# Two attention layers over adjacency graphs: q, k and v products cut into pieces of five and four matmuls, and TensorE's items dealt anew over the steps

## What is computed

```python
h = relu(layernorm(x))                         # before each layer
# layer 0
q, k, v = heads(h @ Wq + bq), heads(h @ Wk + bk), heads(h @ Wv + bv)
s = q @ k.T / sqrt(32) + beta * adj
p = softmax(where(adj > 0, s, -9e15))
x = x + p @ v
# layer 1
q, k, v = heads(h @ Wq.T), heads(h @ Wk.T), heads(h @ Wv.T + bv)
s = q @ k.T * 384 ** -0.5 + (adj + adj)
p = nan_to_num(softmax(where(any(s != 0), s, -inf)))
x = x + (p @ v) @ Wo.T + bo
```

## Time and profile before

| | us |
|---|---|
| profiled execution, as run | 1990.03 |
| its span in the profile | 1988.3 |
| median of three runs | 1988.66 |
| PE, busy | 1900.5 |
| DVE, busy | 1828.6 |
| ACT, busy | 1676.5 |
| POOL, busy | 913.0 |

### The profile page before, as it was taken

How to read it: one execution, slowest core, us unless ns; L and a number is a source line. 1 busy time by engine, 2 the same in 40 slices (tenths; PEclk the granted TensorE clock), 3 DMA queues, 4 the chain that set the end, 5 groups by cost and what they waited for, 6 DMA issues and landing times.

```text
span 1988.3 us, 50014 instructions
## 1 busy us (share of the span) xinstructions
PE 1900.5 (96%) x18336; PEld 1229.1 (62%) x18336; DVE 1828.6 (92%) x3989; ACT 1676.5 (84%) x4275; POOL 913.0 (46%) x1114
## 2 busy tenths in 40 slices
PE   5999999999999999997999999999999999999998
PEld 3566666666666666664666666666666666666665
DVE  5999999999999999997989999999999999999984
ACT  4999999999999999997977887887887888887885
POOL 5465556556655455561353334343343334343331
PEclk9999999999999999998999999999999999999999
DMA  3888999988899898889787788778787788777884
GB/s 134 197 215 220 228 225 234 229 228 223 230 226 230 231 233 226 226 224 225 201 218 198 187 215 222 189 202 210 193 216 194 189 221 211 199 200 202 203 200 113
DMA packets 104723, 415.92 MB, mean 209 GB/s; under 512 B 27008, under 2 KB 31104, under 8 KB 104480
## 3 DMA queue, kind: packets, MB, share of 16 engines
q1 hardware_dynamic: 77728, 305.24, 63.3%
q0 software_dynamic: 26752, 107.49, 18.4%
HBM read 88.61 MB, written 25.17 MB: 57 GB/s over the span
## 4 chain that ended last, share of the span: by engine, by line
PE 49%; DVE 25%; ACT 11%; DMA 6%; SPq 5%; issue 3%; POOL 1%; DVEq 0%; POOLq 0%
DVE s L393 13%; PE sc L248 11%; PE ring L281 11%; DVE pt L406 10%; PE out L340 9%; PE ring L309 6%; ACT s L516 6%; SPq L204 5%; PE ring L265 5%; PE ring L288 4%; DMA pk<-pt 4%; ACT xin L523 2%; PE ring L274 2%; ACT pl L548 1%; PE ring L300 1%
## 5 line engine op out<-in xcount | busy, mean ns | idle before, releaser
L516 ACT ACTIVATE s<-s,nmax 128x512 f32<-128x512 f32 x1536 | 1094.9, 726 | 157.6 <-DVE nmax L393 157.5
L393 DVE CUSTOM_DVE_ANT_0 s<-sc,bias 128x512 f32<-128x512 f32 x1536 | 968.0, 686 | 53.0 <-PE sc L248 25.2
L406 DVE STREAM_TRANSPOSE pt<-s 128x2048 f32<-128x2048 f32 x285 | 656.8, 2304 | 0.0
L248 PE MATMUL sc<-k,q 32*128 32x512 f32 x3072 | 439.9, 642 | 51.0 <-DVE nmax L393 36.2
L516 ACT ACTIVATION_READ_ACCUMULATOR s<-s,nmax 128x1 f32 x1536 | 311.0, 202 | 0.0
L340 PE MATMUL out<-pk,v 128*32 128x192 f32 x6080 | 287.2, 330 | 6.0 <-DMA pk<-pt 6.0
L340 PEld LDWEIGHTS out<-pk,v 128*32 128x32 f32 x6080 | 178.8, 110 | 140.4 <-issue 87.4
L288 PE MATMUL ring<-wv,hT 128*128 128x384 f32 x1152 | 236.3, 349 | 0.0
L281 PE MATMUL ring<-hT,wq 128*128 128x512 f32 x864 | 228.1, 409 | 1.5 <-DVE hT L421 1.5
L281 PE MATMUL ring<-hT,wk 128*128 128x512 f32 x864 | 228.0, 408 | 0.0
L248 PEld LDWEIGHTS sc<-k,q 32*128 32x128 f32 x3072 | 121.5, 184 | 164.0 <-DVE nmax L393 82.8
(11 more groups left out here) (93 smaller groups left out, 1891.4 us busy)
## 6 DMA issues: line engine op xcount, KB each, us to landing
pk<-pt SPq DMA_DIRECT2D x1520, 192.0 KB, 4.9
bias<-in_adj POOLq DMA_DIRECT2D x32, 1024.0 KB, 10.3
res<-in_x POOLq DMA_DIRECT2D x16, 768.0 KB, 7.4
x_between<-res POOLq DMA_DIRECT2D x16, 768.0 KB, 4.5
xin<-x_between POOLq DMA_DIRECT2D x16, 768.0 KB, 10.1
res<-x_between POOLq DMA_DIRECT2D x16, 768.0 KB, 10.6
xin<-in_x POOLq DMA_DIRECT2D x15, 768.0 KB, 9.8
out_x<-res POOLq DMA_DIRECT2D x15, 768.0 KB, 7.0
```

The costliest lines, as they stand in the source:

```text
L248: mm = nc.tensor.matmul(m.sc[:, j, :], m.q[rows, s % 2, P * t:P * (t + 1)], m.k[rows, s % 2, :], start=True, stop=True)
L393: nc.vector.tensor_tensor_reduce(out=m.s[:, t % 2, j, :], in0=m.sc[:, j, :], in1=m.bias[g % 2][:, t, :], scale=s_scale[layer], scalar=3.0e ...
L406: nc.vector.transpose(out=to, in_=m.s[:, t % 2].rearrange("p j (i a e) -> p (j i) a e", a=QUADS, e=HD)).then_inc(turned, 1)
L516: nc.scalar.activation(tile, tile, ACT.Exp, bias=m.nmax[s % 2][:, t, j:j + 1], scale=-1.0, accum_out=m.sums[s % 2][:, t, j:j + 1]).then_in ...
```

## The change

`qk` and `v` get a first piece each, `qk_first` and `v_first`, with places of their own: five of the nine matmuls (`PIECE` = 5). The second piece does the other four into the same bank and then signals. `ring_places` gives the bank to the first piece; it waits for the bank's last reader and the inputs, the second piece waits for nothing. ACT, DVE and POOL skip first pieces. All places of PE's items are new, in both layers, and so are the load steps. The whole of it, with the table of places cut to some rows (layer 0, then layer 1):

```diff
 PLACES = ({
-    "qk": (-2.90, -1.90, 1.10, 2.10, 4.27, 6.10),
-    "v": (-3.50, -0.50, 0.50, 3.50),
+    "qk_first": (-2.93, -1.89, 1.20, 2.11, 5.20, 6.24),
+    "qk": (-2.41, -1.82, 1.38, 2.11, 5.98, 6.33),
+    "v_first": (-3.53, -0.56, 0.80, 3.51),
+    "v": (-3.13, -0.20, 1.71, 3.75),
...
-    "post": (17.50, 17.60, 18.50, 20.60),
+    "post": (17.77, 18.36, 20.07, 20.27),
...
-    "pv": (5.20, 6.70, 8.32, 9.20, 10.70, 12.32, 13.20, 14.70, 16.32),
-    "spread": (7.30, 12.30, 16.61),
+    "pv": (6.31, 7.28, 8.12, 9.31, 10.69, 12.12, 13.86, 14.69, 16.12),
+    "spread": (7.30, 11.62, 14.21),
...
+FIRST = {"qk_first": "qk", "v_first": "v"}
+PIECE = 5
...
-X_STEP, ADJ_STEP, RES_STEP, BIAS_STEPS = 8, (3, 6), (6, 2), (5, 7, 8, 10)
+X_STEP, ADJ_STEP, RES_STEP, BIAS_STEPS = 9, (1, 5), (6, 3), (3, 5, 6, 8)
...
-    ringed = [x for x in OPENING + steps + CLOSING if x[0] != "pv" and x[:2] != ("post", GRAPHS - 1)]
+    ringed = [x for x in OPENING + steps + CLOSING if x[0] not in ("pv", *FIRST.values()) and x[:2] != ("post", GRAPHS - 1)]
     for n, x in enumerate(ringed):
+        result = (FIRST.get(x[0], x[0]), *x[1:])
         slot[x], replaces[x] = n % RING, held[n % RING]
-        held[n % RING] = x
+        slot[result], held[n % RING] = n % RING, result
...
+            def piece(kind):
+                return range(PIECE) if kind in FIRST else range(PIECE, 3 * DT)
...
-                if replaces[kind, g, i]:
+                if replaces.get((kind, g, i)):
...
-                if kind == "qk":
-                    pe.wait_ge(done["hT"], nth("hT", g, DT - 1))
-                    if i < 2 and g % B == 0:
-                        pe.wait_ge(weights_split[i], layer_of(g) + 1)
+                if kind in ("qk_first", "qk"):
+                    if kind == "qk_first":
+                        pe.wait_ge(done["hT"], nth("hT", g, DT - 1))
+                        if i < 2 and g % B == 0:
+                            pe.wait_ge(weights_split[i], layer_of(g) + 1)
                     w, a = (m.wq, m.wk)[i % 2], i // 2
-                    for n, (t, x, y) in enumerate(halves):
+                    for n in piece(kind):
+                        t, x, y = halves[n]
...
-                mm.then_inc(ready[kind], 1)
+                if kind not in FIRST:
+                    mm.then_inc(ready[kind], 1)
```

More of the change, by code:

```diff
@@ L49 @@
 PLACES = ({
-    "hT": (-4.50, -4.40, -4.30),
-    "qk": (-2.90, -1.90, 1.10, 2.10, 4.27, 6.10),
-    "v": (-3.50, -0.50, 0.50, 3.50),
-    "tp": (3.31, 3.32, 3.33, 3.34, 7.31, 7.32, 7.33, 7.34, 11.31, 11.32, 11.33, 11.34),
-    "pv": (5.20, 6.20, 8.20, 9.20, 10.20, 12.20, 13.20, 14.20, 16.20),
-    "post": (17.50, 17.60, 18.50, 20.60),
[L56 to L62, removed]
-    "pv": (5.20, 6.70, 8.32, 9.20, 10.70, 12.32, 13.20, 14.70, 16.32),
-    "spread": (7.30, 12.30, 16.61),
-    "post": (17.50, 17.60, 18.50, 20.50),
-})
+    "hT": (-4.46, -4.36, -4.26),
+    "qk_first": (-2.93, -1.89, 1.20, 2.11, 5.20, 6.24),
+    "qk": (-2.41, -1.82, 1.38, 2.11, 5.98, 6.33),
+    "v_first": (-3.53, -0.56, 0.80, 3.51),
+    "v": (-3.13, -0.20, 1.71, 3.75),
+    "tp": (3.41, 3.48, 3.49, 3.50, 7.33, 7.39, 7.48, 7.48, 11.08, 11.18, 11.26, 11.27),
+    "pv": (5.26, 6.96, 8.47, 9.36, 10.96, 12.28, 13.12, 14.95, 16.20),
+    "post": (17.77, 18.36, 20.07, 20.27),
+}, {
+    "hT": (-4.50, -4.41, -4.30),
+    "qk_first": (-2.92, -1.93, 1.05, 2.07, 4.69, 6.07),
+    "qk": (-2.75, -1.82, 1.25, 2.42, 5.12, 6.10),
+    "v_first": (-3.45, -0.53, 0.74, 3.46),
+    "v": (-3.40, -0.07, 1.20, 3.82),
+    "sums": (0.30, 4.30, 9.76),
+    "zero": (2.09, 5.92, 10.64),
+    "tp": (3.31, 3.32, 3.33, 3.34, 7.31, 7.32, 7.33, 7.34, 11.31, 11.32, 11.33, 11.34),
+    "pv": (6.31, 7.28, 8.12, 9.31, 10.69, 12.12, 13.86, 14.69, 16.12),
+    "spread": (7.30, 11.62, 14.21),
+    "post": (17.30, 17.58, 18.08, 20.41),
+})
+FIRST = {"qk_first": "qk", "v_first": "v"}
+PIECE = 5
 OUT_STEP = ((9, 9, 9), (9, 9, 9))
 STATS_STEP, RELU_STEP = (-12, -8), (-7, -6)
-X_STEP, ADJ_STEP, RES_STEP, BIAS_STEPS = 8, (3, 6), (6, 2), (5, 7, 8, 10)
+X_STEP, ADJ_STEP, RES_STEP, BIAS_STEPS = 9, (1, 5), (6, 3), (3, 5, 6, 8)
 def place(kind, g, i):
@@ L90 @@
     IN_STEP.setdefault(math.floor(at), []).append(x)
-OPENING = [x for kind in ("hT", "qk", "v") for at, x in ITEMS if at < 0 and x[0] == kind]
+OPENING = [x for kinds in (("hT",), ("qk_first", "qk"), ("v_first", "v")) for at, x in ITEMS if at < 0 and x[0] in kinds]
 PER_CHUNK = {"tp": HC, "pv": PARTS, "spread": 1}
@@ L274, in item @@
                         mm = nc.tensor.transpose(to[:, P * t:P * (t + 1)], m.xin[:, t, P * i:P * (i + 1)], m.ident[:])
-                if kind == "qk":
-                    pe.wait_ge(done["hT"], nth("hT", g, DT - 1))
-                    if i < 2 and g % B == 0:
-                        pe.wait_ge(weights_split[i], layer_of(g) + 1)
+                if kind in ("qk_first", "qk"):
[3 more added lines that the diff above has]
+                            pe.wait_ge(weights_split[i], layer_of(g) + 1)
                     w, a = (m.wq, m.wk)[i % 2], i // 2
-                    for n, (t, x, y) in enumerate(halves):
+                    for n in piece(kind):
+                        t, x, y = halves[n]
                         mm = nc.tensor.matmul(to, w[y][:, t, P * a:P * (a + 1)], m.hT[x][:, t, :], start=n == 0, stop=n == 3 * DT - 1)
-                if kind == "v":
-                    if i == 0:
+                if kind in ("v_first", "v"):
+                    if kind == "v_first" and i == 0:
                         pe.wait_ge(done["hT"], nth("hT", g, DT - 1))
@@ L358, in _ @@
                 item(*x)
-                if x == ("v", 0, 0):
+                if x == ("v_first", 0, 0):
                     scores(0, 0, 0)
@@ L415, in item @@
             def item(kind, g, i):
-                if kind == "pv":
+                if kind == "pv" or kind in FIRST:
                     return
@@ L531, in item @@
             def item(kind, g, i):
-                if kind == "pv" or (kind, layer_of(g)) == ("post", 1):
+                if kind == "pv" or kind in FIRST or (kind, layer_of(g)) == ("post", 1):
                     return
```

## The result

| | before | after |
|---|---|---|
| median of the runs, us | 1989.87 (4 runs) | 1974.49 (4 runs, 1972.13 to 1975.07) |
| profiled execution, us | 1990.03 | 1972.13 |

The ratio is 0.9922, its 95% interval 0.9906 to 0.9937. A second set of five runs gave 1974.1 and the same ratio. The forecast of 1989 us and no change was wrong: the kernel is faster by far more than the interval. 1974.49 does lie inside the stated range, 1973 to 2004, but near its lower edge. In a later set one execution of the kernel before took 7751 us, for a reason that nothing here shows; it is left out of every comparison.

What follows compares the result with a forecast made beforehand. It took PE to bound layer 1's steps 4 to 11, and chains over PE, ACT and DVE layer 0. 1990.03 + 5.4 - 5.5 = 1989.9; with the median 1.4 below the profiled run, 1989 us, range 1973 to 2004.

Steps and rivals of the forecast that it cites:

- Sum +0.35 us per graph: Layer 1, steps 4 to 11, PE the bound: cuts and block ends add 0.35 us per graph, +5.4 us (0 to +16).
- the mark that the text set for its refutation: Layer 1: a graph period under 63.3 us would refute the predicted price of the cuts.
- Cuts, +0.1, +0.2 and +0.1: Layer 1: cutting q at the scores +0.1 us, k around a post-product +0.2, v around the spread +0.1.
- zero, +0.1: Layer 1: the small "zero" transpose moves from between full-array blocks to ahead of the scores, +0.1 us per graph.
- post, -0.15: Layer 1: the post-product no longer ends ahead of P-times-v, -0.15 us per graph.
- A spread that leaves step 4 and one that comes into step 11: Layer 1: two spread blocks on PE, 0.41 us each, one leaving and one entering, claimed to change nothing.
- rival 2: Only changes between kinds of block count: 33 stretches for 35 in layer 1, -10.6 us, about 1979; chance 0.12.
- rival 1: Layer 0 gives all: free cuts, waits for h and DMA gone, -0.9 us in 15 graphs, 1976; chance 0.21.
- Rivals 3: Layer 1: each cut and new end costs 0.33, +16 us, with -3 from layer 0: 2002; chance 0.21.
- Rival 4: Layer 1: the residual load comes late, some 1.2 us per graph, +19 us, 2008; chance 0.08.
- Layer 0: Moving q from step 4 to 5 ends ACT's and DVE's waits: -0.35 us per graph, -5.5 us (0 to -14).
- Load steps: Adjacency, bias, x and residual loads at new steps: claimed to cost nothing, covered by about 1 us of slack.

## Why the prediction was wrong

**The step that failed: "Sum +0.35 us per graph", the price of cuts and ends in layer 1, +5.4 us.** Measured: -0.17 to -0.18 a graph; the period of 63.31 is 0.01 above the mark that the text set for its refutation, and far from the 63.6 to 64.1 that it expected. By its terms:

- *Cuts, +0.1, +0.2 and +0.1; zero, +0.1; post, -0.15.* The chains give them all as 0. What costs is the first full-array block behind another kind: q 2.28 there and 2.10 behind a spread, Wo 4.07 and 3.87, Wo with six 2.13 and 1.94, v 1.77 to 1.79 and 1.58 (the first two behind sums or P times v, the last behind Wo). That is 0.18 to 0.21 each time, and scores and P times v take 1.07, 1.44 and 1.01 wherever they stand. Pieces on both sides of the scores pay it once more in q and save it in Wo. I read the prices from starts in the timeline of overlapping blocks, and put them at ends: 0.33 for one ahead of another kind, which is too much, and up to 0.24 where the kind does not change, which is nothing. Whether the 0.19 belongs to the way into full-array work or out of it the sums can't tell, since there are as many ways out as in; the chain, with its modelled ends, puts it at the entry. From the chain through graph 27 before:

```profile
1675.90 0.59 PE ring L300 x4
1676.49 2.10 PE ring L281 x9
...
1705.78 1.77 PE ring L288 x9
```

- *A spread that leaves step 4 and one that comes into step 11, taken as nothing.* The one that leaves gives 0.41 (0.59 less the 0.18 that q then pays itself), and by that steps 5 to 8 became shorter. The one that comes stands inside v's product, ahead of the scores that DVE takes in step 1, and costs 0.44 there. The cut itself costs nothing: v's pieces take 0.97 and 0.71, the whole v 1.67 before. The chain after, and then the row of before:

```profile
1635.34 0.97 PE ring L302 x5
1636.31 0.44 PE ring L314 x4
1636.74 0.71 PE ring L302 x4
```

```profile
1651.97 1.67 PE ring L288 x9
```

So the two spreads did cancel, nearly. The 0.44 less the 0.19 of the next term is the 0.24 by which step 0 grew, and 0.41 less 0.24 is the 0.17 of the period.

- *v from step 9 to step 8* was in no term at all. Its entry, 0.19, is what is left as layer 1's gain, and put back to step 9 it cost 0.34 of 0.36 us a graph (0.21 for its entry, 0.13 for the sums behind it). Moved alone in the kernel before it brought nothing (63.49), though PE held the chain there too: DVE was just behind, and in that run took the chain over from step 9 on.

```profile
1693.12 2.15 PE ring L309 x6
...
1696.44 2.23 DVE pt L406
```

So the Trainium skill, page TensorEngine Tiling (Array Packing), section Key Properties, was the better guide: a change of tiling mode drains the engine. These rows agree for the way into full-array work, by 0.18 to 0.21, and show no price for the other changes of kind but 0.13 at the sums. Over a graph the entries into full-array work fell from 14 to 12, on the chain of steps 4 to 11 from 9 to 8. So of the two changes fewer that **rival 2** counted, one entry counts, 0.19 instead of 0.66; the sign was right, the price a third. That its 1979, and the 1976 of **rival 1**, come near the measured time is luck: layer 0 gave 0.48 a graph and not the 0.9 of rival 1, and graph 17 and the load steps stood in neither. Rivals 3 and 4 fell: layer 1 is shorter, and nothing of DVE waits for the residual. (Rival 4 was also mis-subtracted: 3.1 less 1.4 is 1.7, not 1.2.)

**Layer 0** was right in size: -0.35 a graph forecast, -0.40 measured (-0.48 on the mean, with the packed DMA's waits). The steps hold: the wait for h gone, step 8 shorter by 0.78, step 0 longer by 0.39 with 0.37 more of waiting for scores. The reason was half right. I gave it all to q; moved alone, q made it worse, since the third post was next on ACT's chain. Its three cuts cost 0.3 in a usual graph (55.84 uncut), and 0.03 on the mean of the fifteen: among them is one entry more where step 9's q stands around P times v (1.35 + 1.13 for 2.29 in the chains of graph 10).

**Load steps, "Cost nothing":** they seem to bring 4 us, by a way that stays open. **Graph 17**, -4.1, was not foreseen at all: I read one usual graph of each layer and multiplied, and never looked at the turn between the layers. Put back one at a time: layer 0 -8.1, layer 1 with graph 17 -4.0, load steps -3.7, for -15.4 measured.

The other marks. In layer 1: the post's wait 0.52 instead of under 0.4, PE busy 62.89 instead of over 63, the wait for h 1.64, over 1 as said. In layer 0: the period 56.13 and the wait for h as said, the wait for the scores of step 1 0.74 instead of 0.3 to 0.6.

## What to carry to other kernels

Price a block by the chain of waits, not by starts of overlapping rows, and see which neighbour it has: in these kernels a cut or a move cost PE time only where it made a new entry into full-array work from another kind of matmul. When a wait is taken away, find what is second on the same chain and move both, and look at what each moved item does to the queue of every engine that handles its result. Where a pipeline has a turn between two phases, read that graph by itself.

## What was not expected of the hardware

The first full-array block behind 32-row or 32-column matmuls took 0.18 to 0.21 us more in the chains (1.58 and 1.79 for the same nine matmuls of v), the way back nothing, but for the sums: 0.35 behind v, 0.22 behind P times v. Matmul ends are modelled in the profile, but DVE's steps, which are not PE's records, show the two together: step 0 took 4.49 us for 4.15. The adjacency's load (1024 KB) took 12.7 us from issue to first use in graph 9 of the kernel after (542.15 to 554.89) and 12.6 when it was issued 3 us later (545.08 to 557.65): the later issue reached the waiting POOL nearly in full. The executions of one kernel in one set lie 2 to 13 us apart, and two profiles of the kernel after differ in the opening (30.8 and 28.7) and in graphs 15 and 16 (128.0 and 131.2), while the sums over the usual graphs agree to 0.1: single parts of the program can be compared far more finely in a profile than the whole can in its time.
